# Turning the normalised input by VectorE blocks and a round trip through DRAM instead of TensorE, and moving one softmax scaling from ScalarE to VectorE

## The reference

```
x = x + layernorm(attention(layernorm(x)))            # 8 heads of 64, causal softmax, sinusoidal table added to q and k
x = x + layernorm(tanh(layernorm(x) @ W1 @ W2 @ W3 + bias))
```

## Time and profile before

| | |
|---|---|
| median of three runs | 553.28 us |
| the profiled execution | 553.95 us |
| its span in the profile | 552.1 us |
| busy in the span: PE, PEld, DVE, ACT, POOL | 94%, 79%, 74%, 86%, 68% |
| mean granted TensorE clock | 0.985 of full speed |

### The profile page before, as it was taken

The page is one execution under the profiler, slowest core; times in us unless marked ns, Lnnn a source line. Parts: engine busy times, 40 slices in busy tenths (PEclk is TensorE's granted clock), DMA queues, the critical chain, the costliest instruction groups (busy, mean ns, idle before and its releaser), DMA issues.

```text
span 552.1 us, 18676 instructions
## 1 busy us (share of the span) xinstructions
PE 519.4 (94%) x5396; PEld 435.5 (79%) x5396; DVE 410.6 (74%) x1967; ACT 476.3 (86%) x1732; POOL 375.3 (68%) x650
## 2 busy tenths in 40 slices
PE   8599999999999999999999999999999999999984
PEld 5478888888888888888888888888888888888762
DVE  4567777788777778877777787777778777777743
ACT  3688999999999999899999989999998999999941
POOL 3435677777677777767777776777777677776544
PEclk9789999999999999999999999999999999999989
DMA  5000001110010011100001010000110011000001
GB/s 162 29 3 20 12 23 29 30 29 29 10 29 22 26 29 29 29 10 29 24 23 29 29 29 10 29 28 19 29 29 29 10 29 29 19 19 21 21 1 29
DMA packets 27964, 14.57 MB, mean 26 GB/s; under 512 B 1699, under 2 KB 27430, under 8 KB 27942
## 3 DMA queue, kind: packets, MB, share of 16 engines
q1 hardware_dynamic: 26982, 13.57, 8.7%
q10 hardware_dynamic: 960, 0.72, 0.4%
HBM read 10.09 MB, written 4.19 MB: 26 GB/s over the span
## 4 chain that ended last, share of the span: by engine, by line
PE 74%; DVE 12%; issue 8%; ACT 3%; DMA 1%; DVEq 1%; POOL 0%; SPq 0%; POOLq 0%; ACTq 0%
PE scores L879 15%; PE turned_and_heads L936 14%; PE misc_bank L1007 11%; PE turned_and_heads L922 10%; PE qk_bank L897 5%; PE qk_bank L898 4%; PE qk_bank L899 4%; DVE scores L642 3%; PE misc_bank L865 3%; PE misc_bank L979 2%; ACT pt L300 2%; DVE heads_t L666 2%; DVE neg_max L642 2%; DVE qk L652 2%; PE misc_bank L866 2%
## 5 line engine op out<-in xcount | busy, mean ns | idle before, releaser
L269 ACT ACTIVATE probs<-scores,neg_max 128x256 f32<-128x256 f32 (+1 forms) x512 | 209.6, 452 | 4.7 <-DVE neg_max L642 4.7
L642 DVE CUSTOM_DVE_ANT_0 scores<-scores,mask 128x256 f32<-128x256 f32 (+1 forms) x512 | 165.5, 390 | 24.5 <-PE scores L879 24.2
L652 DVE TENSOR_TENSOR qk<-qk_bank,pe 128x512 f32<-128x512 f32 x128 | 87.3, 682 | 60.5 <-PE qk_bank L899 60.4
L269 ACT ACTIVATION_READ_ACCUMULATOR probs<-scores,neg_max 128x1 f32 x512 | 121.7, 238 | 0.0
L434 POOL TENSOR_TENSOR probs<-probs,inv_sum 128x512 f32<-128x512 f32 x126 | 101.7, 828 | 12.7 <-DVE inv_sum L658 12.7
L936 PE MATMUL turned_and_heads<-pt,vals 128*64 128x256 f32 (+1 forms) x1024 | 98.6, 335 | 12.0 <-ACT pt L300 12.0
L298 ACT COPY pt<-turned_and_heads 128x512 f32<-128x512 f32 x128 | 74.9, 585 | 40.2 <-PE turned_and_heads L922 40.2
L879 PE MATMUL scores<-qk 64*128 64x256 f32 (+1 forms) x1024 | 100.5, 335 | 0.0
L936 PEld LDWEIGHTS turned_and_heads<-pt,vals 128*64 128x64 f32 x1024 | 67.1, 138 | 40.5 <-issue 14.2
L281 ACT ACTIVATE probs<-probs,inv_sum 128x256 f32<-128x256 f32 (+1 forms) x256 | 95.5, 451 | 0.7
L879 PEld LDWEIGHTS scores<-qk 64*128 64x128 f32 x1024 | 87.6, 192 | 4.7 <-issue 0.2
(11 more groups left out here) (91 smaller groups left out, 850.2 us busy)
## 6 DMA issues: line engine op xcount, KB each, us to landing
x_in<-in_x SPq DMA_DIRECT2D x32, 128.0 KB, 2.2
x_res<-in_x SPq DMA_DIRECT2D x32, 128.0 KB, 2.1
out_x<-x SPq DMA_DIRECT2D x32, 128.0 KB, 1.9
w_raw<-in_w_qkv_t SPq DMA_DIRECT2D x2, 256.0 KB, 4.6
w_raw<-in_w_qkv_t ACTq DMA_DIRECT2D x1, 256.0 KB, 4.1
pe<-pe_table SPq DMA_DIRECT2D x1, 256.0 KB, 6.1
wo<-in_w_o_t ACTq DMA_DIRECT2D x1, 256.0 KB, 6.8
mask<-causal_mask ACTq DMA_DIRECT2D x1, 128.0 KB, 5.8
```

Source lines behind the costliest of these rows:

```text
L269: ins = nc.scalar.activation(probs[k][j][:, h, lo:hi], s_bank[j][:, h, lo:hi], ACT.Exp, bias=neg_max[k][j][:, i:i + 1], scale=-1.0, accum_ ...
L642: ins = nc.vector.tensor_tensor_reduce(some, some, mask[:, t * P:2 * P], -1.0, HIGHEST, ALU.add, ALU.min, neg_max[k][j][:, i:i + 1])
L652: nc.vector.tensor_tensor(qk[j][:, :], qk_bank[:, :], pe[:, :], ALU.add).then_inc(qk_kept, 1)
```

## The change

The normalised x of every batch but the first no longer goes through TensorE. DVE transposes it in blocks of 32 by 32 (`turn_x_blocks`, one instruction over 128x256), SP writes the blocks in four DMAs to a place in DRAM where they lie as the full transpose, with runs of 32 floats (`send_x`), waits for all four, and reads the 128 KB back into `xt` (`read_x`). `keep_x_hi` and `keep_x_lo` then read `xt` in SBUF in place of `misc_bank`. The waits that kept `misc_bank` for the turned x go.

`scale_probs` for the first pair of unit 1 moves from ACT to DVE, in four `tensor_scalar` instructions with one factor for each row. Unit 0's stays on ACT.

The order of the steps is written anew in every engine's `slot`, `begin` and `end`. The final normalisation of the feed-forward part (`stats_ffn`, `norm_ffn`) now runs one batch later.

```diff
+            def send(b, blocks, to, sent):
+                for j in range(P // 32):
+                    r = slice(32 * j, 32 * (j + 1))
+                    place = to[b.parity][:, :, r].rearrange("(i p) t c -> p t i c", p=32)
+                    sp.dma_start(place, blocks[b.parity][r, :, :].rearrange("p t (i c) -> p t i c", c=32)).then_inc(sent[b.parity], 16)
+            def send_x(b):
...
+                sp.wait_ge(x_blocked, b.times(1))
+                send(b, x_blocks, x_rows, x_sent)
+            def read_x(b):
...
+                sp.wait_ge(x_sent[b.parity], moves(b, 1) * 64)
+                sp.dma_start(xt[b.parity][:, :, :], x_rows[b.parity]).then_inc(x_moved[b.parity], 16)
             def slot(b, k):     # SP
+                if k == 0:
+                    load_x(b.plus(3))
+                    send_x(b.plus(2))
+                else:
+                    read_x(b.plus(2))
+                    store(b.plus(-3))
+                    load_res(b.plus(1))
...
+            def scale_probs(b):     # DVE
+                dve.wait_ge(inv_found, pairs(b, 1, 1))
+                for t, (lo, hi) in enumerate(((0, T), (T, SC))):
+                    for h in range(2):
+                        some, i = probs[1][0][:, h, lo:hi], 2 * t + h
+                        ins = nc.vector.tensor_scalar(some, some, inv_sum[1][0][:, i:i + 1], None, ALU.mult)
+                ins.then_inc(scaled_first[1], 1)
+            def turn_x_blocks(b):
...
+                dve.wait_ge(norms["x"]["normed"], b.times(1, 1))
...
+                nc.vector.transpose(x_blocks[b.parity][:, :, :], xn[b.parity][:, :, :]).then_inc(x_blocked, 1)
```

More of the change, by code:

```diff
@@ L201, in load, with load_x @@
                 sp.dma_start(dst[b.parity][:, :, :], rows(x_dram, b)).then_inc(loaded[b.parity], 16)
-            def slot(b, k):
[L204 to L215, removed]
+            def load_x(b):
+                if not b.exists() or b.is_below(2):
+                    return
+                wait(sp, norms["x"]["normed"], b.times(1, -1))
+                load(b, x_in, x_loaded)
@@ new lines, in load_res @@
+            def load_res(b):
+                if not b.exists():
+                    return
+                wait(sp, x1_made, b.times(1, -1))
+                load(b, x_res, res_loaded)
+            def send(b, blocks, to, sent):
[3 more added lines that the diff above has]
+                    sp.dma_start(place, blocks[b.parity][r, :, :].rearrange("p t (i c) -> p t i c", c=32)).then_inc(sent[b.parity], 16)
@@ L693, in slot @@
+                    stats_x(b.plus(2))
+                    take_moments("attn", b.plus(-2))
                 else:
                     wait_stats("x", b.plus(2))
+                    keep_heads(b.plus(-1), 0)
+                    take_moments("x", b.plus(2))
+                    norm_attn(b.plus(-2))
+                    keep_qk(b, 1, 1)
+                    invert_sums(b, 0, 1)
+                    keep_x_lo(b.plus(1))
+                    stats_y(b.plus(-2))
                     wait_stats("y", b.plus(-2))
-                    keep_heads(b.plus(-1), 0)
+                    row_max(b, 1, 0)
@@ L788, in begin @@
                 take_w_rest(1)
+                stats_x(first.plus(1))
+                wait_stats("x", first.plus(1))
+                take_moments("x", first.plus(1))
                 take_w_rest(2)
@@ L1013, in slot @@
                 if k == 0:
-                    make_qk(b, 1, 0)
-                    make_heads(b.plus(-1), 0)
-                    make_vals(b, 1)
                     make_qk(b, 1, 1)
@@ L1020, in slot @@
                     turn_probs(b.plus(-1), 1, 1)
-                    turn_x(b.plus(1))
-                    turn_y(b.plus(-2))
-                    make_heads(b.plus(-1), 1)
-                    make_ffn(b.plus(-2))
-                    make_qk(b.plus(1), 0, 0)
-                else:
-                    make_attn(b.plus(-1), 0)
-                    make_attn(b.plus(-1), 1)
-                    make_qk(b.plus(1), 0, 1)
+                    make_qk(b.plus(1), 0, 0)
+                    make_vals(b, 1)
+                    make_heads(b.plus(-1), 1)
+                    make_qk(b.plus(1), 0, 1)
+                else:
+                    turn_y(b.plus(-2))
                     turn_probs(b, 0, 0)
@@ L1032, in slot @@
                     turn_probs(b, 0, 1)
+                    make_ffn(b.plus(-2))
+                    make_qk(b.plus(1), 1, 0)
+                    make_attn(b.plus(-1), 0)
+                    make_attn(b.plus(-1), 1)
+                    make_heads(b, 0)
                     make_vals(b.plus(1), 0)
```

215 lines of the change are left out of this document (114 added, 101 removed).

## The result

The changed kernel takes 543.94 us (median of 4 runs, 543.11 to 545.04), the kernel before 553.46 beside it (552.21 to 553.7): ratio 0.9834 [0.9807, 0.986], 1.7% faster. The forecast was 532 with a range of 523 to 548. The sign and the range hold; of 21.4 us that were to be gained 9.5 came.

The account below looks back on a forecast made before the run. TensorE's program plus its gaps was taken as the bound. Thirty batches falling from 16.05 to 15.37 us gave 20.4, the fill 1, the drain 0: 553.95 - 21.4 = 532.5, taken as 532; range 523 to 548.

Parts of the forecast that it names:

- The sum of TensorE's program, 15.22: TensorE's steps of one batch at the old order's prices, 15.50 us, less 0.28 for turn_x.
- VectorE's 14.3: VectorE's work per batch: 12.58 plus 1.25 for scalings and 0.45 for the block transpose, 93% of 15.37 us.
- the 1.75 a batch of waits: VectorE's waits for TensorE's projections, 35.9 us in 20 batches, claimed as room for 1.7 us of new work.
- Rival A: DMA round trip of x lands late, beyond 7.7 us, and stalls ScalarE: 571 us at 9; chance 0.10.
- Rival B: GpSimd delays VectorE's four scalings by 0.3 to 0.6 us each: period about 15.8, time 545; chance 0.2.
- the sign for B: On VectorE, tensor_scalar above 0.5 us in the median, or bimodal.
- The change on TensorE: Section on TensorE's program: turn_x and the make_heads gap go, 0.15 us of gaps stay, period 15.37.
- Three slacks of about 0.2: Tight places in TensorE's new order: turn_probs(b,0,0), second half of scores(b+1,0), turn_y; allowed 0.15 us of gaps a batch.
- What would show it: List of signs: right if batches start 15.2 to 15.5 us apart; wrong above 15.8 or below 15.2.
- rival C: Gaps return at the three slacks on TensorE, only turn_x's 0.28 a batch is gained: 545 us; chance 0.13.
- The fill: Start of the kernel: batch 1's x statistics come earlier and its way leads past TensorE; 1 us gained (0 to 3).
- the bound of 9 us: Upper bound of x's DMA round trip, if each small piece costs three times a row of 512 B; estimate 5.4.

Follow-up runs that it names:

- h1: f1 with ScalarE's tanh ahead of keep_turned(b,0,1), unit 1's scaling staying on VectorE: 531.28 us, ratio 0.9593.
- g1: f1 with e3's edit on top, unit 1's scaling back on ScalarE and tanh ahead of the copy: 530.75 us, ratio 0.9612.
- e4: The changed kernel with two further 128x128 transposes on TensorE in each batch, result unread: 548.93 us, ratio 0.9931.
- f3: The kernel before with only unit 1's scaling moved to VectorE, behind keep_qk at the end of slot 1: 581.37 us, ratio 1.0516.
- e3: The changed kernel with unit 1's scaling back on ScalarE and tanh moved ahead of a copy: 539.07 us, ratio 0.9748.
- e2: The changed kernel with VectorE's beginning in the old order, batch 1's statistics behind the first keep_qk: 541.49 us, ratio 0.9788.
- e1: The changed kernel with attention's moments ahead of x's statistics on VectorE: 536.58 us, ratio 0.9695.
- f4: The kernel before with only x's turn by block transpose and DMA round trip, blocks behind keep_qk on VectorE: 563.15 us, ratio 1.0192.
- h2: The kernel before with only unit 1's scaling moved to VectorE, ahead of keep_qk(b+1,0,1): 555.2 us, ratio 1.0041.
- f2: f1 with GpSimd's program written out without its loop: 534.42 us, ratio 0.9661.
- g2: f1 with TensorE's turn_y moved between turn_probs(b,0,0) and the scores: 543.49 us, ratio 0.9832.
- f1: The changed kernel with attention's moments ahead of x's statistics and VectorE's old beginning together: 533.87 us, ratio 0.9656.

## Why the prediction was wrong

**Right, step by step.** The sum of TensorE's program, 15.22: the batches without a gap take 15.21 (h1) and 15.23 (g1). That the sum came out is luck in its parts. Its prices were of the old order, and a step's price depends on the step ahead of it. A projection that starts a make_qk costs 0.12 behind make_vals and 0.32 behind turn_probs or make_heads (h1):
```profile
278.05 0.12 PE qk_bank L979
...
281.07 0.32 PE qk_bank L979
```
In the new order two of the four make_qk are of the dear kind, so they take 2 x 0.70 + 2 x 0.91 = 3.22 for 2.88. Make_vals behind a make_qk takes 0.69 and not 0.89, 1.59 for 1.78 in the two; make_heads takes 2.90 for 2.97 and turn_y 0.22 for 0.28. The errors cancel. The 0.28 for turn_x, too, is 0.22 by e4. The gap in front of make_heads is gone. ScalarE's 13.4: 110.46 / 128.5 x 15.75 = 13.5. VectorE's 14.3: 115.78 / 128.5 x 15.75 = 14.2; the four scalings took 1.0 alone and up to 1.4 in steady batches, the estimate was 1.25; the block transpose 0.41 for 0.45.

Two slips in the working change nothing here: the 1.75 a batch of waits is 35.9 us over 20.5 batches (over 20 it is 1.80), and 30 x 0.83 + 3 off 553.3 gives 525 and not the range's 523.

Rival A: the four issues took 2.61 us (0.65 each, not 0.40) and from the first one to the landing of the read it is 268.35 + 2.0 - 264.36 = 6.0 for 5.4, within the 7.7:
```profile
264.36 2.61 SPq L243 DMA_DIRECT2D x_rows<-x_blocks  x4
268.35 0.34 SPq L258 DMA_DIRECT2D xt<-x_rows  x1
```
ScalarE's cast of that batch starts at 272.18, 1.8 later; only once, in the fill, does it wait for the read (1.4 us).

Rival B: VectorE's instructions do get longer. A scaling of 128x256 takes 531 ns in the mean, above the 0.5 of the sign for B, where it takes 346 in f3; keep_x_lo went from 424 to 595, but it also reads two tiles in SBUF now and not one. Yet h1 against g1 shows that it isn't on the path: with the scaling on VectorE or not, 531.28 and 530.75.

**The step that failed** is the last of "The change on TensorE": "Three slacks of about 0.2 mean that I can't expect none of them to be missed. I take 0.15 us of gaps". They are 0.53, nearly the 0.57 of before; the period of 15.75 is just inside the 15.2 to 15.8 of "What would show it". Only one of the three slacks is missed, turn_y (0.23 a batch); turn_probs(b,0,0) and scores(b+1,0) run without a gap (280.36 and 280.88 in the chain, 0.52 and 1.36). The two other gaps are at places that weren't on the list: make_attn behind tanh, 0.15 in every batch, and the second half of scores(b,1), 0.145, which waits for keep_qk(b,1,1) behind norm_attn.

I had laid out TensorE and looked for tight places from one producer back. Of the chain behind them, attention's copy, statistics, moments, root and norm, I had written "A rough estimate for that way is 9 us", for a slack of 0.2. From the end of make_attn to the start of turn_y it is 279.93 - 270.20 = 9.73 in the slow batch, 264.01 - 254.69 = 9.32 in the other, where the layout had room for 9.23. The first half of the same chain ends at scores(b,1): by the layout its second half is due at 1.24 + 0.68 = 1.92, or 15.22 - 12.84 + 1.92 = 4.30 behind make_attn, and it started 274.57 - 270.20 = 4.37 behind it. That sum I hadn't made. And tanh's bank is a wait for a reader, which no flow of data shows. The outcome is near rival C, with its price of 545, which had 0.13, though C too had the gaps at the three slacks. That the time still fell into the range is owed to the range's reach over the rivals and not to the forecast's mechanism.

**The fill** was to bring 1 us and cost 1 in the two profiles, but these have different clocks there. At 0.87 from 10 to 50 us the kernel before has the scores of batch 3 at 68.12 and e3, with the changed kernel's beginning, at 67.75. So the gain was about 0.4 for 1, and the rest is the clock, which the sum had no term for. What held the gain down is that x's statistics of batch 1 stand ahead of keep_qk(first, 0, 0), 1.1 to 1.7 by e2's table; I had looked only at what the path of batch 1 gains by that.

**The sum then:** 21.4 forecast; the period gained 0.33 in 28 rather than 0.68 in 30, 20.4 - 9.2 = 11.2 less; the fill 2.0 less; the drain 0.7 more: 8.9 in the span. The last two hold for these two profiles and are of the clock's size. With the two orders of VectorE and the one of ScalarE mended the kernel is at 531.3, the forecast of 532, and only turn_y's wait in every second batch is left, 0.15 a batch, as much as I had allowed for all gaps. What lies between 532 and 544 is three orders of a few instructions: by the periods 6.5 (e1) and 4.3 (tanh), and some 1.3 in the fill (e2), 12.1 of the 12.7.

**A step that came out only by the new order.** "its waits for projections were 35.9 us in 20 batches, 1.75 a batch, and these 1.7 us go into that room": f3, f4 and h2 show that idle time is a place and not an amount. Behind the keep_qk at its end everything on VectorE stood on the path at full price (1.03 a batch for 1.00 of work, 0.33 for 0.36), ahead of it about a tenth (2.5 us against 28.9).

**Small writes.** The 32 KB in runs of 128 B land in 2.0 us, the store of 128 KB in 1.9, and in the steady part no engine waits for them but SP, which issues them. By the trace a packet of 128 B took 13 ns in the mean and one of 512 B 28, so a quarter of the bytes cost half the time, where the bound of 9 us had three times the time. The Trainium skill (DMA: Bandwidth & Descriptors, Specifications) has transfers below 512 B as read-modify-write; 13 ns against 28 shows the lower rate by the byte, and no price of it reaches the time.

## What to carry to other kernels

Where one engine bounds at 97%, a change is worth what it takes from that engine's program less the waits that its new order makes, and each wait has to be followed through all engines down to the thing that starts it, the readers of a shared bank too; a slack of 0.2 us that rests on a rough estimate is no slack. Idle time on another engine is room only ahead of the instruction that ends it. Price a step behind the step that it will follow, not behind the one that it follows now. Before taking a new order, look in the chain for "issue" rows of 0.1 us and compare the instruction behind each with the same one elsewhere: here three of them were 0.53 us of each batch, and two changes of order took 0.39 of that away, 11 us. And before a few us are put down to an edit, compare the granted clock of the fill and the drain: here the four runs of f2 part by it, 532.5 and 533.0 from 535.9 and 536.6.

## What the runs showed of the hardware

- A matmul that starts behind a wait is longer in the chain than one that follows another: turn_y 0.43 for 0.22, make_attn 2.05 for 2.00. So a wait of 0.12 costs up to 0.33.
- A full-size projection that follows matmuls on part of the array takes 0.32 from start to start, behind another full-size one 0.12 (h1).
- One full-size pair of transposes among matmuls on part of the array costs 0.3 us more than beside other full-size ones (g2).
- tensor_scalar of 128x256 fp32 with a factor for each row and its neighbour of 128x128, twice: 1.0 us in all in f3, 1.34 in the changed kernel, where GpSimd is at work on most of that time (531 against 346 ns for the 128x256); ScalarE's four take 1.39. The block transpose of 128x256 fp32 takes 0.41.
- A DMA with four dimensions and runs of 128 B takes 0.65 to issue, where the store's takes 0.40 and the plain read back 0.34. Its packets of 128 B take 13 ns, those of 512 B 28.
- The granted clock of the fill differs between executions of one kernel, and 0.87 for 0.96 from 10 to 50 us is 2.4 to 2.6 us (e2's table).
- The end of a loop's body on GpSimd seems worth up to 0.3 us, once for each pass of two batches: f1's periods alternate, 15.37 and 15.66, and with GpSimd's loop written out (f2) most are 15.38 and 15.44. The path by which the loop's end delays turn_y was not followed.
